# A triangular inverse by doubling: a signal of its own for the update of the plain inverse

## What is computed

```python
def step(S, inp):
    rt, dt, kt, vt, kkt, at = inp
    sa = jnp.einsum('bhvk,bhk->bhv', S, -kkt)
    S = S * dt[:, :, None, :] + sa[..., None] * (kkt * at)[:, :, None, :] + vt[..., None] * kt[:, :, None, :]
    y = jnp.einsum('bhvk,bhk->bhv', S, rt)
    return (S, y)
```

## Time and profile before

| | before |
|---|---|
| median of 3 runs | 2785.02 us (2784.21 to 2785.96) |
| the profiled execution, its own time | 2783.87 us |
| its span in the profile | 2781.9 us |
| PE busy, of the span | 2546.8 us, 92% |
| DVE busy, of the span | 1944.4 us, 70% |
| ACT busy, of the span | 1281.9 us, 46% |
| mean granted clock of PE | 0.976 of full speed |

### The profile page before, as it was taken

The page is one execution under the profiler, slowest core; times in us unless marked ns, Lnnn a source line. Parts: engine busy times, 40 slices in busy tenths (PEclk is TensorE's granted clock), DMA queues, the critical chain, the costliest instruction groups (busy, mean ns, idle before and its releaser), DMA issues. The chain is left out here.

```text
span 2781.9 us, 67593 instructions
## 1 busy us (share of the span) xinstructions
PE 2546.8 (92%) x26848; PEld 1811.2 (65%) x26848; DVE 1944.4 (70%) x3760; ACT 1281.9 (46%) x1945; POOL 78.0 (3%) x94
## 2 busy tenths in 40 slices
PE   6999999998999896799999999999959999999999
PEld 4777777777777775233333333333249999999998
DVE  6777777777777773798888888888445555656554
ACT  3333333333333330256666666666734454454544
POOL 0000000000000000110000000000050000000000
PEclk9999999999999997799999999999979999999999
DMA  2000000000000000311101102110030001010100
GB/s 73 14 25 24 21 21 21 21 21 21 23 24 23 24 20 16 88 35 47 54 13 58 38 25 58 30 37 10 11 117 28 27 30 32 24 36 21 38 19 27
DMA packets 138289, 90.26 MB, mean 32 GB/s; under 512 B 68544, under 2 KB 130624, under 8 KB 138048
## 3 DMA queue, kind: packets, MB, share of 16 engines
q1 hardware_dynamic: 136448, 81.34, 10.3%
q0 software_dynamic: 1600, 5.24, 0.6%
HBM read 56.89 MB, written 29.36 MB: 31 GB/s over the span
## 5 line engine op out<-in xcount | busy, mean ns | idle before, releaser
L1246 DVE TENSOR_REDUCE a_mx<-a_pm 128x1 f32<-128x512 f32 (+3 forms) x1120 | 709.2, 672 | 144.7 <-PE a_pm L1144 83.1
L1228 ACT ACTIVATE a_pt<-a_sc 128x1024 f32<-128x1024 f32 (+3 forms) x640 | 544.9, 897 | 360.2 <-PE a_sc L1168 188.1
L1144 PE MATMUL a_pm<-a_ka,a_qa 96*128 96x512 bf16 (+3 forms) x1280 | 401.9, 354 | 15.9 <-DMA a_qa<-q_scratch 11.7
L1165 PE MATMUL a_sc<-a_qa,a_ka 98*128 98x512 bf16 (+3 forms) x1280 | 354.2, 349 | 29.0 <-ACT a_pt L1228 18.5
L1144 PEld LDWEIGHTS a_pm<-a_ka,a_qa 96*128 96x128 bf16 x1280 | 123.3, 97 | 307.1 <-DVE a_mx L1246 214.1
L1184 PE MATMUL a_po<-a_pt,a_v_st 128*32 128x512 f32 (+3 forms) x2560 | 300.9, 542 | 0.1
L1771 DVE TENSOR_TENSOR e_h_lo<-v_all,e_h_hi 128x512 fp32r<-128x512 f32 x208 | 145.9, 702 | 189.4 <-ACT e_h_hi L1618 188.2
L1165 PEld LDWEIGHTS a_sc<-a_qa,a_ka 98*128 98x128 bf16 x1280 | 116.7, 98 | 147.0 <-ACT a_pt L1228 58.8
L1616 ACT ACTIVATE v_all<-e_ps 128x512 f32<-128x512 f32 x176 | 103.5, 588 | 124.1 <-PE e_ps L1508 123.4
L1508 PE MATMUL e_ps<-e_h_hi,e_e_l_hi 128*128 128x256 f32 x512 | 147.7, 288 | 0.0
L1508 PE MATMUL e_ps<-e_h_lo,e_e_l_hi 128*128 128x256 f32 x512 | 144.8, 283 | 0.0
(11 more groups left out here) (314 smaller groups left out, 5512.0 us busy)
## 6 DMA issues: line engine op xcount, KB each, us to landing
a_ka<-k_scratch SPq DMA_DIRECT2D x192, 64.0 KB, 2.3
a_qa<-q_scratch SPq DMA_DIRECT2D x192, 64.0 KB, 2.3
o_scratch<-a_o_sb SPq DMA_DIRECT2D x32, 256.0 KB, 2.6
v_all<-o_scratch SPq DMA_DIRECT2D x256, 32.0 KB
q_scratch<-r_q_part SPq DMA_DIRECT2D x192, 32.0 KB, 1.8
k_scratch<-r_k_part SPq DMA_DIRECT2D x192, 32.0 KB, 1.5
r_x_tok<-in_x SPq DMA_DIRECT2D x32, 128.0 KB, 2.1
s_scratch<-r_s_tok SPq DMA_DIRECT2D x32, 128.0 KB, 1.7
```

What stands on the lines that cost most here:

```text
L1144: last = mm(out[:, at_:at_ + width], qa[b][0:NP, qc, h0 + i, 128 * (qt % 4):128 * (qt % 4) + 128], ka[b][0:NP, h0 + i, 512 * kc:512 * kc + ...
L1165: last = mm(sc[x][:, y, off:512], ka[b][:, h, 128 * j:128 * j + 128], qa[b][:, qc, h, off:512], start=True, stop=not diag)
L1228: nc.scalar.activation(pt[x][g % 2][:, :, off:512], sc[x][:, :, off:512], ACT.Exp).then_inc(s_p[x], 1)
L1246: ve.tensor_reduce(mx[:, h0:h0 + heads, qt, kc:kc + 1].rearrange("p h o -> p (h o)"), pm[:, k % RING, 0:heads * width].rearrange("p (h w) ...
```

## The change

The plain step gets a signal `s_plain`, and the first add a signal `s_plainsb`. PE waits for the first add alone ahead of the next z, and for the second add only ahead of the next plain and transposed steps. DVE no longer waits for the transposed step ahead of the first add; it waits for the plain step there, and between the adds it waits for its own first add and for the transposed step.

```diff
+        s_plain, s_plainsb = sig("plain_step", LEVELS - 2), sig("plain_kept", LEVELS - 2)
...
                 for lev in range(LEVELS - 1):
                     if lev:
-                        pe.wait_ge(s_invsb.sem, s_invsb.at(t, lev))
+                        pe.wait_ge(s_plainsb.sem, s_plainsb.at(t, lev))
                     else:
                         pe.wait_ge(s_first.sem, s_first.at(t, 2))
                     pairwise(4, am[:, :, 0, :], inv).then_inc(s_z.sem, s_z.up())
                     give_way()
                     pe.wait_ge(s_zsb.sem, s_zsb.at(t, lev + 1))
                     if lev == 0:
                         pe.wait_ge(s_base.sem, s_base.at(t, 2))
+                    else:
+                        pe.wait_ge(s_invsb.sem, s_invsb.at(t, lev))
                     if lev < LEVELS - 2:
-                        pairwise(5, invT, zz)
+                        pairwise(5, invT, zz).then_inc(s_plain.sem, s_plain.up())
                     pairwise(6, zz, invT).then_inc(s_inv.sem, s_inv.up())
                     give_way()
...
                     give_way()
+                    if lev < LEVELS - 2:
+                        dve.wait_ge(s_plain.sem, s_plain.at(t, lev + 1))
+                        ve.tensor_tensor(flat(inv), flat(inv), ps[:, 5, :], ALU.add).then_inc(s_plainsb.sem, s_plainsb.up())
+                        dve.wait_ge(s_plainsb.sem, s_plainsb.at(t))
                     dve.wait_ge(s_inv.sem, s_inv.at(t, lev + 1))
-                    if lev < LEVELS - 2:
-                        ve.tensor_tensor(flat(inv), flat(inv), ps[:, 5, :], ALU.add)
                     ve.tensor_tensor(flat(invT), flat(invT), ps[:, 6, :], ALU.add).then_inc(s_invsb.sem, s_invsb.up())
                     dve.wait_ge(s_invsb.sem, s_invsb.at(t))
```

More of the change, by code:

```diff
@@ L285, in _ @@
         def _(pe):
-            back_signals, tail_signals = (s_am, s_z, s_inv, s_g, s_u, s_sn, s_y), (s_mean, s_gvar, s_out)
+            back_signals, tail_signals = (s_am, s_z, s_plain, s_inv, s_g, s_u, s_sn, s_y), (s_mean, s_gvar, s_out)
             for q in back_signals + tail_signals:
@@ L682, in _ @@
         def _(dve):
-            back_signals = (s_amsb, s_base, s_first, s_zsb, s_invsb, s_state, back_step)
+            back_signals = (s_amsb, s_base, s_first, s_zsb, s_plainsb, s_invsb, s_state, back_step)
             tail_signals = (s_yc, s_yg, tail_step)
```

## The result

| | before | after |
|---|---|---|
| median of the runs | 2784.61 us (2781.14 to 2785.96, 6 runs) | 2768.89 us (2762.51 to 2775.45, 6 runs) |
| the profiled execution, its own time | 2783.87 us | 2767.11 us |
| its span | 2781.9 us | 2765.1 us |
| mean granted clock of PE in the profile | 0.976 | 0.978 |

The ratio is 0.994, with a 95% interval of 0.992 to 0.996. The kernel is faster by 0.6%, 15.7 us by the medians, where 11.7 were forecast. Run again later beside other kernels it gave 2772.83 us and a ratio of 0.9947 (0.9927 to 0.9967). The changed kernel ran 12 times in all, with 2770.9 us and 0.9789.

The account below looks back on a forecast made before the run. PE was taken to bound the looped turns, busy 839.84 of 926.00 us. A + B + C = 3.9 + 3.6 + 4.2 = 11.7 us, taking the median from 2785.0 to 2773.3 us, range 2767 to 2781.

Parts of the forecast that it names:

- Term A: Looped turns: DVE's earlier first add brings zz3 0.60 us earlier and removes PE's wait ahead of plain3; 3.9 us gained.
- Term B: Last turn: the waits of z1, z3 and z4 go, with part of z3's returning ahead of plain3; 3.6 us gained.
- Term C: Last turn: with stops ahead of z1 and z4 gone, two slow stretches reach PE's upper clock; 4.2 us, between 0 and 5.4.
- The first stretch: Last turn, plain1 and transposed1 at clock 0.67: expected at the upper level, 1.4 us less.
- the one of level 3: Last turn, plain3 and transposed3 at clock 0.58: its 1.2 us not counted, since the stop ahead of plain3 grows.
- The third: Last turn, transposed4 with the first chunk products at clock 0.53: expected at the upper level, 2.8 us less.
- The costs put at nothing: PE's count and second wait, up to 3.2 us, and DVE's wait between the adds, 4.2 at most: both taken as nothing.
- the clock of the looped turns: The xg and xw projections behind z0 may run at the lower clock more or less often: 4.9 us either way, nothing summed.
- Rivals 1 to 4: Last turn's clock unchanged, 0.22; only last turn gains, 0.13; slower, second wait holds PE's queue, 0.04; nothing happens, 0.05.

Follow-up runs that it names:

- the filled kernel before: Kernel before the change, with three unused matmuls of constants added in PE's 1.5 us stop ahead of z0: 2779.83 us, ratio 0.9976.
- the two filled kernels: Kernel before and changed kernel, each with three unused matmuls of constants in PE's stop ahead of z0: 2779.83 and 2769.99 us.
- the run with it alone: Changed kernel with the new signals used only in the last turn, the other 15 turns as before: 2780.93 us, ratio 0.9990.
- the run with PE's half alone: Changed kernel, but DVE's first add waits for the transposed step again; z still waits for the first add alone: 2792.61 us, ratio 1.0025.
- the runs with the looped turns alone: Changed kernel with the new signals only in turns 0 to 14, the last turn as before: 2772.49 us, ratio 0.9958.
- two longer turns: Changed kernel with one front matmul 384 or 512 columns wide in place of 256, no instruction added: 2772.10 and 2776.10 us.
- the run with repeated products: Changed kernel with the first two pairs' products at level 1 made twice, 4 matmuls more every turn: 2786.95 us, ratio 1.0012.

## Why the prediction was right

**Term A** had the right mechanism and was too small by a fifth. The first add lies under the transposed step, zz3 starts 0.60 us earlier behind transposed2, and the waits for zz3 went to nothing; PE itself is late next. The prediction took the idle time as the cost, 3.9 us (its own product is 4.0). What came back is 5.0, since without the stop plain3 also overlaps the end of the key projection. The same 5.0 stand in all ten profiles of kernels in which DVE's first add is early in the looped turns.

**Term B** came as it stood: the waits of z1, z3 and z4 are gone, and of z3's 1.47 us 1.00 came back ahead of plain3 (1.02 to 2.02), where 0.87 were expected. By starts it is 4.0 us, where 3.6 were forecast, again with the overlap.

**Term C** had the right size in the profile, but in part by luck. From the last z0 to attention it is 7.8 us, as B + C were, which leaves 3.8 for C. The first stretch, plain1 and transposed1, gave 1.3 of the 1.4 forecast, and the one of level 3 stayed low as forecast. The third gave only 0.6 of 2.8: transposed4 is at the upper level now, but z4 ahead of it takes 1.66 in place of 1.15, and the first chunk products are still at the lower one. What it lacked was gained where nothing was forecast: 1.1 at z0 and plain0, and 0.9 in a product of the tail (L512, 1.98 us, now L515, 1.13). The part at z0 and plain0 is chance, since the changed kernel's second profile has them as slow as before. That transposed4 and the tail's product run at the upper level is no chance, since all nine profiles with the change have it. The reason that the prediction gave for the first stretch, two stops close together, is not enough by itself, as the filled kernel before has both stops there and no lower level behind them. Between the two filled kernels, where that stretch is at the upper level in both, the last turn differs by 4.4 us, hardly more than B. Over the timed runs the last turn's share stays unsure, as the run with it alone shows. The Trainium skill, TensorE: Matmul & The Clock Gate, "What's actually happening", says that where the level changes is free of the kernel's start. The trace agrees: `xg` and `xw` took 40.3 us in one profile of the changed kernel and 43.6 in another.

**The costs put at nothing** were nothing in this kernel: no stop of PE stands at the plain steps with two waits, other than for zz, and taking out DVE's wait between the adds changes no time that can be told. The Trainium skill, VectorE: DVE Perf Modes, "The DRAIN you can't avoid", has a semaphore between vector operations as free. Here the measurement differs: the second of two adds starts 0.11 to 0.13 us later when it waits for the first, and in the run with PE's half alone this lay on the path, 0.12 a turn.

**What was mis-sized** is the clock of the looped turns. The prediction had "nothing in the sum" for it, with 4.9 us either way. In the first profile `xg` and `xw` alone gave 6.5, in the second 3.2. In the runs with the looped turns alone, whose last turn is as before, the mean clock rose by 0.0029 from 0.9760; among the 86 runs of the kernel before, 0.001 of the mean clock goes with 2.0 us, so this is some 5.8 us, an estimate. With the 5.0 of A it makes 10.8 of the 11.7 us of the looped turns alone; the rest lies within the interval.

Rivals 1 to 4 fell: the clock of the last turn rose in the profiles (plain1, transposed1 and transposed4 at the upper level in all nine), the looped turns gained, no second wait held PE up, and something happened.

**What stays open** is why the looped turns run at the lower level less. It is not the length of the turn, as two longer turns kept the better clock. The seven kernels in which zz3 comes in time and which add no more than one matmul have clocks from 0.9782 to 0.9808; the three without fill in which plain3 waits have 0.9760 to 0.9762. But the run with repeated products has no such wait and still 0.9762, with the stop of 15.1 us among the products. That a stop of 0.27 us in the middle of the turn decides about stretches behind z0 was not shown.

## What to carry to other kernels

Where two results leave one engine and a second engine takes them one after the other, a signal for each lets the second engine work under the first one's second step; look for the gain not at the wait that the signal replaces but at whatever the second engine is late for further on. Price a stop by the distance from start to start and not by the idle time alone: here the stop of 0.27 us cost 0.33 a turn. Before you trust a sum of waits to the microsecond, look at what the clock does behind PE's stops, and time a change of this size by several runs: here the twelve runs of the changed kernel lay 17 us apart, further than the change itself. One profile can agree with a sum by luck; look at the same rows in every profile that you have. Filling a stop with idle matmuls raised the clock here, but the fill cost as much as the clock gave back.

## What had not been expected

- Matmuls added to PE's loop lengthened a stop of PE elsewhere in the loop, for which the profile shows no release: 5.5 us in the changed kernel, 7.7 with one matmul more in a turn, 11.9 and 15.1 with three, 15.1 with four. Widening a matmul left it at 8.2 and 4.1, and without added matmuls it lies between 5.0 and 7.4. That it goes with the number of instructions fits these numbers. A longer stop is not all a cost: with four matmuls more the chunk products take 11.2 us longer, with three more only 2.6 and 2.7. What PE waits for there was not shown.
- Half of a change that helps made the kernel slower: a new wait of 0.13 us lay on the path there, and no cost of it can be told beside the other half.
